# Sorting a router's batches in a fused LoRA and top-2 MoE kernel: the experts' first positions summed on VectorE, the batches' numbers packed at the first singles

## The reference

```python
x = x + (x @ W_base.T + b_base + 2.0 * lora(x, w=cond_8))      # layer 0, 8 LoRA experts of rank 16
rw = softmax(cond_8); w, sel = top_k(rw, 2); w = w / w.sum(-1) # a batch picks two of 8 experts
out = sum over e of dense_w[b, e] * mlp(x[b], gate_e, up_e, down_e)
out = out + mlp(x, shared_gate, shared_up, shared_down)        # the shared expert, all batches
x = x + out                                                    # mlp: gelu(x@gate) * (x@up) @ down, 128 -> 512 -> 128
```

## Time and profile before

| | before |
|---|---|
| median of 3 runs | 131.17 us (130.94 to 131.41) |
| the profiled execution | 130.85 us |
| its span | 129.2 us |
| PE busy | 124.9 us (97%), 873 matmuls |
| DVE busy | 90.2 us (70%) |
| ACT busy | 72.0 us (56%) |
| POOL busy | 61.8 us (48%) |
| PEclk, all 40 slices | 9 of 9 |
| bytes moved | 26.56 MB, mean 206 GB/s |

### The profile page before, as it was taken

One profiled execution on the slowest core, in us unless ns is written; L12 is line 12 of the kernel. 1 busy time (PEld: TensorE's weight loads), 2 busy tenths in 40 slices (PEclk: granted clock), 3 DMA queues, 4 the chain that ended last, 5 costly groups with the idle time before them and its releaser, 6 DMA issues.

```text
span 129.2 us, 3167 instructions
## 1 busy us (share of the span) xinstructions
PE 124.9 (97%) x873; PEld 113.9 (88%) x873; DVE 90.2 (70%) x177; ACT 72.0 (56%) x136; POOL 61.8 (48%) x111
## 2 busy tenths in 40 slices
PE   6999999999999999999999999999999999999991
PEld 5948887878887888998999999999999999999990
DVE  1686798769979999633377768667867686766731
ACT  2349677976956877113466485648565846711110
POOL 5364974463797877453344632643364604610000
PEclk9999999999999999999999999999999999999999
DMA  2998778799100077679745686558699960014922
GB/s 39 266 329 313 218 272 219 296 310 292 36 3 0 5 173 239 233 275 411 302 183 223 244 322 231 208 223 325 228 315 306 402 211 0 3 26 141 263 82 61
DMA packets 14524, 26.56 MB, mean 206 GB/s; under 512 B 2224, under 2 KB 7600, under 8 KB 12976
## 3 DMA queue, kind: packets, MB, share of 16 engines
q1 hardware_dynamic: 14048, 26.28, 60.8%
q10 hardware_dynamic: 464, 0.13, 0.4%
HBM read 12.52 MB, written 1.31 MB: 107 GB/s over the span
## 4 chain that ended last, share of the span: by engine, by line
PE 97%; issue 0%; DVE 0%; DVEq 0%
PE bank L1059 11%; PE bank L1100 9%; PE bank L1101 9%; PE bank L1099 9%; PE bank L1081 6%; PE bank L1004 6%; PE bank L1005 6%; PE bank L1006 6%; PE bank L1121 5%; PE bank L1122 4%; PE bank L1123 4%; PE bank L1022 3%; PE bank L928 3%; PE bank L936 3%; PE bank L1023 3%; PE bank L1024 3%
## 5 line engine op out<-in xcount | busy, mean ns | idle before, releaser
L558 ACT ACTIVATE work<-bank 128x512 f32<-128x512 f32 x48 | 28.7, 599 | 38.3 <-PE bank L1101 17.6
L720 DVE TENSOR_TENSOR bank<-bank,work 128x512 f32<-128x512 f32 x40 | 27.9, 698 | 18.3 <-PE bank L1101 13.1
L739 DVE TENSOR_TENSOR hT_lo<-bank,hT_hi 128x512 fp32r<-128x512 f32 x40 | 27.3, 682 | 1.0 <-issue 0.5
L1099 PE MATMUL bank<-xp,wst 128*128 128x256 f32 x96 | 27.2, 284 | 0.0
L1101 PE MATMUL bank<-xp,wst 128*128 128x256 f32 x96 | 27.2, 283 | 0.0
L1100 PE MATMUL bank<-xp,wst 128*128 128x256 f32 x96 | 27.2, 283 | 0.0
L485 POOL TENSOR_TENSOR wstd<-wexd,wstd 128x512 fp32r<-128x512 f32 x12 | 15.6, 1296 | 24.0 <-ACT wstd L600 24.0
L567 ACT CAST hT_hi<-bank 128x512 fp32r<-128x512 f32 x40 | 23.3, 583 | 1.8 <-DVE bank L720 1.8
L1099 PEld LDWEIGHTS bank<-xp,wst 128*128 128x128 f32 x96 | 18.4, 192 | 0.0
L1100 PEld LDWEIGHTS bank<-xp,wst 128*128 128x128 f32 x96 | 18.4, 192 | 0.0
L1101 PEld LDWEIGHTS bank<-xp,wst 128*128 128x128 f32 x96 | 18.4, 192 | 0.0
(11 more groups left out here) (156 smaller groups left out, 214.0 us busy)
## 6 DMA issues: line engine op xcount, KB each, us to landing
wst<-wex SPq DMA_DIRECT2D x12, 1024.0 KB, 5.0
raw_ex<-n_L_cond_skill_gate_dram SPq DMA_DIRECT2D x8, 256.0 KB, 3.5
raw_ex<-in_L_cond_skill_up_dram SPq DMA_DIRECT2D x8, 256.0 KB, 4.1
sst<-n_L_cond_skill_gate_dram SPq DMA_DIRECT2D x8, 256.0 KB, 3.5
sst<-in_L_cond_skill_up_dram SPq DMA_DIRECT2D x8, 256.0 KB, 4.0
xn<-in_x_dram SPq DMA_DIRECT2D x4, 256.0 KB, 4.8
out_dram<-xT SPq DMA_DIRECT2D x4, 256.0 KB, 2.7
sst<-_L_cond_shared_gate_dram SPq DMA_DIRECT2D x1, 256.0 KB, 4.9
```

Source lines behind the costliest of these rows:

```text
L558: act.activation(gelu_sb[q], gate_ps[q][:, :], ACT.Gelu_apprx_tanh).then_inc(gelu_done, 1)
L720: dve.tensor_tensor(up_ps[u][:, :], up_ps[u][:, :], gelu_sb[q], ALU.mult).then_inc(h_done, 1)
L739: dve.tensor_tensor(hT_lo[:, q, :], up_ps[u][:, :], f32(hT_hi[:, q, :]), ALU.subtract).then_inc(lo_done, 1)
L1099: pe.matmul(of_c, w_hi, x_hi, start=True, stop=False)
```

## The change

The first positions of the experts no longer go through TensorE. VectorE makes twos and what is odd for the 8 experts (three ops at chunk 0 of group 0), multiplies both by a table `below` (2 or 1 for the experts in front, 0 for the rest; nine columns, the ninth sums all) and reduces along the experts (three ops at chunk 1). GpSimd takes up from there with six ops. `sort_counts` now spreads the counts to all 16 rows, so that each partition can sum for itself. Of the packs only two_e and four_e stay in group 3; two_b, slot_eb and four_b come behind the last group's sum (`pack_batches`), six_b behind gated_single(1) (`pack_slots`).

```diff
         def _(pool):
...
-            pool.memset(upick[:, :, :], 2.0).then_inc(const_fill, 1)
+            pool.memset(below[:, 0, :, :], 2.0).then_inc(const_fill, 1)
+            pool.memset(below[:, 1, :, :], 1.0).then_inc(const_fill, 1)
...
-            pool.affine_select(out=upick[:, 0, :], in_=upick[:, 0, :], compare_op=ALU.is_gt, fill=0.0,
-                               base=0, pattern=[[1, 8]], channel_multiplier=-1).then_inc(consts, 1)
...
+            for i in range(2):
+                pool.affine_select(out=below[:, i, :, :], in_=below[:, i, :, :], compare_op=ALU.is_gt, fill=0.0,
+                                   base=0, pattern=[[1, 9], [-1, 8]], channel_multiplier=0).then_inc(consts, 1)
...
-            pool.wait_ge(sort_sum, 2)
-            pool.tensor_scalar(par[:, :], half[:, :], -2.0, None, ALU.mult).then_inc(sort_step, 1)
-            pool.wait_ge(sort_step, 4)
-            pool.tensor_tensor(par[:, :], par[:, :], rank_n[:, 1, :], ALU.add).then_inc(sort_step, 1)
-            pool.wait_ge(sort_sb, 2)
-            pool.tensor_tensor(pos_e[:, 0, :], rank_n[:, 0, 0:8], starts[:, 2, :], ALU.subtract).then_inc(sort_step, 1)
...
+            pool.wait_ge(sort_sum, 5)
+            pool.tensor_tensor(pos_e[:, 1, :], rank_n[:, 0, 0:8], starts[:, 0, 0:8], ALU.add).then_inc(sort_step, 1)
+            pool.tensor_scalar(pos_e[:, 2, :], starts[:, 1, 0:8], starts[:, 0, 8:9], None, ALU.add).then_inc(sort_step, 1)
...
-                    if g == 0 and c == 2:
-                        act.wait_ge(sort_mm, 2)
-                        act.copy(starts[:, :, :], start_ps[0:B, 0:24].rearrange("p (a b) -> p a b", a=3)
-                                 ).then_inc(sort_sb, 1)
...
                     if g == 0 and c == 0:
...
-                        dve.tensor_reduce(half[:, :], n_ge[:, :, :], AXIS_X, ALU.add).then_inc(sort_sum, 1)
+                        dve.tensor_reduce(twos_odd[:, 0, :], n_ge, AXIS_X, ALU.add).then_inc(sort_sum, 1)
+                        dve.wait_ge(sort_sum, 2)
+                        dve.scalar_tensor_tensor(twos_odd[:, 1, :], twos_odd[:, 0, :], -2.0, n, ALU.mult, ALU.add
+                                                 ).then_inc(sort_sum, 1)
+                    if g == 0 and c == 1:
+                        dve.wait_ge(sort_sum, 3)
+                        dve.tensor_tensor(in_front, twos_odd[:, :, :].rearrange("p i (a e) -> p i a e", a=1)
+                                          .to_broadcast([B, 2, 9, 8]), below[:, :, :, :], ALU.mult).then_inc(sort_sum, 1)
+                        dve.wait_ge(sort_sum, 4)
+                        dve.tensor_reduce(starts[:, :, :], in_front, AXIS_X, ALU.add).then_inc(sort_sum, 1)
+
+                        dve.scalar_tensor_tensor(pos_e[:, 0, :], twos_odd[:, 0, :], 2.0, rank_n[:, 0, 0:8],
+                                                 ALU.mult, ALU.is_equal).then_inc(sort_sum, 1)
...
-                        pack(two_b[:, 1:17], idx[:, 32:64:2], B, idx[:, 33:64:2])
-                    if g == 3 and c == 1:
-                        dve.wait_ge(packs, P_TWO_B)
-                        pack(slot_eb[:, :], idx[:, 0:LEFT:2], B * B, two_b[:, 1:1 + NP])
...
+            def pack_batches():
+                dve.wait_ge(packs, P_PAD)
+                pack(two_b[:, 1:17], idx[:, 32:64:2], B, idx[:, 33:64:2])
+                dve.wait_ge(packs, P_TWO_B)
+                pack(slot_eb[:, :], idx[:, 0:LEFT:2], B * B, two_b[:, 1:1 + NP])
+                pack(four_b[:, :], two_b[:, 1 + NP:17:2], B * B, two_b[:, 2 + NP:17:2])
...
             sum_group(NG - 1)
-            dve.wait_ge(packs, P_SIX_B)
+            pack_batches()
+            dve.wait_ge(packs, P_FOUR_B)
             first = of_four(read(dve, four_b, 0, B ** 4))
             gated_single(1)
+            pack_slots()
             add_single(0, first[0])
...
-            def sort_starts():
-                pe.wait_ge(sort_sum, 2)
-                pe.wait_ge(sort_step, S_PAR)
-                pe.wait_ge(x1lo_ready, NG)
-                pe.matmul(start_ps[0:B, 0:24], half[:, :], upick[:, :, :].rearrange("p a e -> p (a e)"),
-                          start=True, stop=False)
-                pe.matmul(start_ps[0:B, 8:16], par[:, :], ltri[:, 0:8], start=False, stop=True).then_inc(sort_mm, 1)
...
             def sort_singles():
                 pe.wait_ge(sort_step, S_CLASS)
+                pe.wait_ge(x1lo_ready, NG)
...
                     elif g == 1:
-                        pe.wait_ge(sort_sb, 2)
+                        pe.wait_ge(x1lo_ready, NG)
...
-                    if g == 0 and c == 2:
-                        sort_starts()
```

More of the change, by code:

```diff
@@ L78, in lora_then_top2_moe @@
         ltri = sb("ltri", [B, B])
-        upick = sb("upick", [B, 3, 8])
+        below = sb("below", [B, 2, 9, 8])
         memb = sb("memb", [B, 2, B])
@@ L82, in lora_then_top2_moe @@
         rank_n = sb("rank_n", [B, 2, B])
-        n_ge = sb("n_ge", [B, B, 8])
-        half = sb("half", [B, B])
-        par = sb("par", [B, B])
-        starts = sb("starts", [B, 3, 8])
+        twos_odd = sb("twos_odd", [B, 2, 8])
+        starts = sb("starts", [B, 2, 9])
         pos_e = sb("pos_e", [B, 4, 8])
@@ L94, in lora_then_top2_moe @@
         rows = sb("rows", [B, 2, 3, 32])
+        spare = rows[:, :, :, :].rearrange("b k v n -> b (k v n)")
+        n_ge = spare[:, 0:64].rearrange("b (e r) -> b e r", e=8)
+        in_front = spare[:, 0:144].rearrange("b (i f e) -> b i f e", i=2, f=9)
         wlist = sb("wlist", [P, 32])
@@ L143, in lora_then_top2_moe @@
         count_ps = bank[3]
-        start_ps = bank[6]
         rank_ps = bank[7]
@@ L245, in read @@
             return eng.value_load(table[0:1, bass.ds(n, 1)], min_val=0, max_val=top - 1)
-        P_PAD, P_TWO_B, P_SLOT_EB, P_TWO_E, P_FOUR_E, P_FOUR_B, P_SIX_PART, P_SIX_B = range(1, 9)
-        S_MEMB, S_PAR, S_POS, S_CLASS, S_ROWS = 3, 5, 11, 16, 32
+        P_PAD, P_TWO_E, P_FOUR_E, P_TWO_B, P_SLOT_EB, P_FOUR_B, P_SIX_PART, P_SIX_B = range(1, 9)
+        S_MEMB, S_POS, S_CLASS, S_ROWS = 3, 9, 14, 30
         block = ctx.enter_context(nc.Block())
@@ L356, in _ @@
                       allow_small_or_imprecise_dtypes=True).then_inc(consts, 1)
-            pool.wait_ge(consts, 8)
+            pool.wait_ge(consts, 7)
             pool.wait_ge(rt_step, 4)
@@ L789, in shared_group @@
                         dve.tensor_copy(idx[:, :], list_ps[0:1, 0:64]).then_inc(lists_ready, 1)
+                    if g == 3 and c == 1:
                         dve.wait_ge(lists_ready, 2)
-                        dve.wait_ge(packs, P_PAD)
-                        pack(two_b[:, 1:17], idx[:, 32:64:2], B, idx[:, 33:64:2])
-                    if g == 3 and c == 1:
-                        dve.wait_ge(packs, P_TWO_B)
-                        pack(slot_eb[:, :], idx[:, 0:LEFT:2], B * B, two_b[:, 1:1 + NP])
                         pack(two_e[:, :], idx[:, LEFT:LEFT + NS:2], E, idx[:, LEFT + 1:LEFT + NS:2])
@@ L799, in shared_group, with pack_slots @@
                         pack(four_e[:, :], two_e[:, 0:4:2], E * E, two_e[:, 1:4:2])
-                        pack(four_b[:, :], two_b[:, 1 + NP:17:2], B * B, two_b[:, 2 + NP:17:2])
-                    if g == 3 and c == 3:
-                        pack(six_b[:, :], two_b[:, 0:NP:3], B * B, two_b[:, 1:NP:3])
-                        dve.wait_ge(packs, P_SIX_PART)
-                        pack(six_b[:, :], six_b[:, :], B * B, two_b[:, 2:NP:3])
+            def pack_batches():
[4 more added lines that the diff above has]
+                pack(four_b[:, :], two_b[:, 1 + NP:17:2], B * B, two_b[:, 2 + NP:17:2])
+            def pack_slots():
+                pack(six_b[:, :], two_b[:, 0:NP:3], B * B, two_b[:, 1:NP:3])
+                dve.wait_ge(packs, P_SIX_PART)
+                pack(six_b[:, :], six_b[:, :], B * B, two_b[:, 2:NP:3])
             def add_single(s, b):
@@ L878, in _ @@
             last = of_four(read(dve, four_b, 1, B ** 4))
+            dve.wait_ge(packs, P_SIX_B)
             dve.wait_ge(sum_done, NG)
@@ L940, in sort_counts @@
             def sort_counts():
[L942 removed]
+                pe.wait_ge(consts, 7)
                 pe.wait_ge(sort_step, S_MEMB)
                 pe.matmul(count_ps[0:B, 0:B], ltri[:, :], memb_sum[:, :], start=True, stop=True)
[L945 to L953 removed]
+                pe.matmul(count_ps[0:B, B:2 * B], ones[:, 0:B], memb_sum[:, :], start=True, stop=True).then_inc(sort_mm, 1)
             def sort_singles():
                 pe.wait_ge(sort_step, S_CLASS)
+                pe.wait_ge(x1lo_ready, NG)
                 pe.matmul(rank_ps[0:B, 0:2], ltri[:, :], twice[:, 0:2], start=True, stop=True)
```

58 lines of the change are left out of this document (26 added, 32 removed).

## The result

| | before | after |
|---|---|---|
| median, runs side by side | 130.94 us (6 runs) | 130.14 us (129.99 to 130.5, 6 runs) |
| ratio | | 0.994 (95% interval 0.9929 to 0.9951) |
| profiled execution, its span | 130.85, 129.2 us | 130.35, 128.6 us |
| matmuls, PE busy | 873, 124.9 us | 869, 124.0 us |

The forecast was 130.75 with a range of 130.4 to 131.25. So there are two questions: what the changed rows are worth, and why the worth differs.

What follows compares the result with a forecast made beforehand. TensorE's own work was taken as the bound (97% of the span, 0% waiting). -0.40 + 0.08 - 0.10 + 0 = -0.42 us off the median of 131.17 gave 130.75 us, range 130.4 to 131.25.

Steps and rivals of the forecast that it cites:

- Part 1: Group 0, TensorE: two small sort matmuls leave, and all their cost goes, -0.40 us (bounds 0.35 to 0.45).
- Part 2: Group 0, chunk 1: three new VectorE ops make hT_lo late for the second down group, +0.08 us (bounds 0, +0.3).
- the rule's extra 0.1: Group 0: gate_lo(0) may lose to a GpSimd op, making chunk 2's hT_lo late; sum -0.32 instead of -0.42 us.
- Part 3: Group 3: five packs leave VectorE, so the last hT_lo comes in time for TensorE, -0.10 us (bounds 0 and -0.15).
- I see no transfer that TensorE waits for: Behind group 0: TensorE itself releases everything, loads included, so the gain is not given back at a fixed time.
- Part 4: First singles: the moved packs and register read delay gated_single(1), but within TensorE's slack, 0 us (upper bound +0.2).
- rival of the slower kind: Group 0: the three VectorE ops take 1.5 us and TensorE waits, +0.48 us, 131.65 us; chance 0.10.
- The sum: Whole kernel: the terms give -0.42 us, taken off the median of 131.17 for 130.75 us.

Runs made afterwards that it cites:

- pair_back: The changed kernel with two small 16-row matmuls put back on TensorE ahead of the first down product, result unused: 130.51 us, ratio 0.9960 to before.
- sort_only: The kernel before with only the sort's sums moved to VectorE, all seven packs left in group 3: 130.42 us, ratio 1.0004.
- again_after: The changed kernel run once more, no edit: 130.11 us, ratio 0.9977 to before; its profiled execution took 129.96 us.
- before_4: The kernel before, unchanged, one more profiled execution, in which VectorE started ahead of GpSimd near 38 us and two_b took 1.18 us: 131.25 us.
- again_before: The kernel before, unchanged, profiled a second time: that execution took 130.12 us.
- before_2: The kernel before, unchanged, one more profiled execution, with a step of 0.64 us to the first single: 130.97 us.
- before_3: The kernel before, unchanged, one more profiled execution: 130.30 us.
- packs_only_2: The kernel before with only the packs moved, the sort as before, a repeat: 130.50 us, ratio 1.0001.
- after_4: The changed kernel run again, no edit: 130.28 us, ratio 0.9934 to before; its profiled execution took 130.50 us.
- call A: Follow-up comparison on one chip of before (130.42 us, 29 runs) with the changed kernel (130.11) and each half of the change alone (130.42 and 130.28).
- call D: Follow-up comparison on one chip: before 130.93 us (17 runs), before with the copy of idx moved 130.93, the changed kernel 130.28.
- call E: Follow-up comparison on one chip: before 130.37 us (23 runs), before with three pack operands from PSUM 130.28, before with only the packs moved 130.33.
- best: The changed kernel with all packs in group 3, three reading PSUM, idx copied ahead of hT_lo, one group 0 VectorE op moved later: 129.72 us, ratio 0.9946.
- before_idx: The kernel before with the copy of idx ahead of hT_lo at chunk 0 of group 3: 130.93 us, ratio 0.9995.

## Why the prediction was right in direction and too small

**Part 1 (-0.40).** Right: 0.40 on TensorE's rows, 0.36 by pair_back. But "all of it goes" was true only with the packs out of the way; sort_only kept none of it. I had VectorE full in group 3 and did not ask what happens there when TensorE comes 0.4 us earlier and GpSimd, whose part of the sort ends sooner, earlier still: its sum started 0.02 us behind two_b in before, 0.35 ahead of it in sort_only.

**Part 2 (+0.08).** Right: +0.05. GpSimd lost against gate_lo(0), not the other way round (its L408 took 0.72 us), so the rule's extra 0.1 did not come.

**Part 3 (-0.10, bounds 0 and -0.15).** This is the step that failed: what the packs cost in group 3 was mis-sized. It was priced from one execution in which two_b took 0.17 us, with GpSimd's sum starting 0.02 us behind it. I quoted slot_eb, held up to 0.72 us beside GpSimd's op, and did not look at what stood beside two_b. What the runs show in its place: beside the moved sort, taking the packs out was worth 0.31 us, three times the term (sort_only 130.42, again_after 130.11), and in the order of before_4 the packs cost 0.85 us of the stretch. The bound should have been about -0.85, not -0.15. The 0.10 itself, the late last load at 51.38, is in the profile before and in before_4 only; again_before, before_2 and before_3 lose no step there.

**"I see no transfer that TensorE waits for"** was wrong. The profile before had the first single's load ready exactly in time: the step was 0.23 us. I took a wait of zero for slack. The issue of the transfer did move with the copy of idx, as I had said (1.22 us behind it in before and after), but its time to landing scatters by 0.5 us (3.3 to 3.8). Both kernels pay for that: before_2 lost 0.41 us, packs_only_2 0.27, after 0.2, after_4 0.34.

**Part 4 (0).** Right: gated_single(1) was held by the register read and TensorE did not wait for it. No rival of the slower kind came up either: the three VectorE ops took 0.62 us.

**The sum.** The result lies 0.61 us below the forecast. 0.23 of that is the base: I took the saving off a median of 131.17 from three runs, without asking why it was 0.3 us above the profiled execution, and the six runs of the comparison have 130.94. The other 0.38 is the saving, -0.80 in place of -0.42. Where before is in the order of its first profile, the stretches of four executions of each kernel are 110.23 and 109.92 on average, -0.31, and call A gives -0.31: the -0.35 of group 0, and nothing sure from the end of group 3. That -0.42 lies so near to -0.31 is luck, since the two halves taken alone gave 0 and -0.14 in that call. The rest of the -0.80 in the first comparison is likely the other order, which Part 3 left out; that stays open, since none of the timed runs at 130.93 was profiled.

## What to carry to other kernels

Where two engines start long ops within a few hundredths of a microsecond of each other, a profile shows one of two kernels. Look for such ties before pricing anything behind them, and bound the price by both orders. A small op that reads two SBUF tiles beside a busy GpSimd can be held until GpSimd's op ends (two_b, 0.97 us for 16 numbers); take one operand from PSUM, or move it. And a wait of zero is not slack: ask of every engine and transfer that is just in time what happens when it comes a few tenths later, or its consumer earlier.

## What the runs showed that I had not expected

- The order of two engines' instructions, set by 0.04 us at 38 us, moved the end of the kernel by 0.85 us. The time of the kernel before falls by the chip: none of 17 timed runs below 130.84 us in call D, 19 of 23 below 130.8 in call E. Whether it is this order that falls so, and why, is open.
- TensorE's first instructions take 0.42 us or 0.27 us (the transpose of w_nat) while PEclk reads 9 in both; when they get short differs between executions by some 3 us. The first shared matmul starts between 15.22 and 15.78 us, but not by this alone: best, where they are short from 5 us on, starts it at 15.51, and before_idx, where they are still long at 6 us, at 15.29. What sets either moment stays open.
- The pair of 16-row matmuls, 0.2 us of work by its rows, costs 0.40 us between 512-column matmuls even with its operands long there.
